# A one-core vision tower with eight experts: the scratch is cleared first, all expert rows are loaded at once, and the first experts' weights are asked for one after the other

## The reference

```
h = patchify(x) @ W_proj.T + b_proj + pos_emb          # 16 x 36 patches of 768 -> 256
h = concat(cls_tok, h)                                 # 16 x 37 = 592 tokens
h = h + attention(layernorm(h))                        # 16 heads of 16, causal, b_qkv, W_out, b_out
x = layernorm(h)
gates = softmax((x @ w_red) @ normalised(wg).T)        # 8 experts
e, score = argmax(gates), max(gates)
h = h + score * (gelu(x @ w1[e] + b1[e]) @ w2[e] + b2[e])   # 256 -> 1024 -> 256
```

## Time and profile before

| | us |
|---|---|
| median of 3 runs | 144.17 (144.15 to 144.57) |
| the profiled execution, its own time | 144.8 |
| its span, first to last recorded work | 143.0 |
| PE busy | 128.5 (90% of the span) |
| DVE, ACT, POOL busy | 58.2, 48.1, 41.0 |
| moved by DMA | 33.38 MB, mean 233 GB/s |

### The profile page before, as it was taken

How to read it: one execution, slowest core, us unless ns; L and a number is a source line. 1 busy time by engine, 2 the same in 40 slices (tenths; PEclk the granted TensorE clock), 3 DMA queues, 4 the chain that set the end, 5 groups by cost and what they waited for, 6 DMA issues and landing times.

```text
span 143.0 us, 2701 instructions
## 1 busy us (share of the span) xinstructions
PE 128.5 (90%) x1024; PEld 109.0 (76%) x1024; DVE 58.2 (41%) x179; ACT 48.1 (34%) x143; POOL 41.0 (29%) x53
## 2 busy tenths in 40 slices
PE   5999999999849999999879999992999999999970
PEld 2787888777536778777679988991899989999850
DVE  1012997619813788879847001600212111120210
ACT  0300004465712646562339350263006060505100
POOL 8600044900074093304637500040002020202022
PEclk9999999999995999999999999999689999999998
DMA  4999999948849999999104648885978799400000
GB/s 151 369 263 409 393 371 389 408 175 180 143 108 168 212 361 382 360 396 347 46 0 183 231 119 267 336 299 165 376 242 337 260 300 352 153 5 22 2 26 28
DMA packets 19790, 33.38 MB, mean 233 GB/s; under 512 B 1783, under 2 KB 13560, under 8 KB 19774
## 3 DMA queue, kind: packets, MB, share of 16 engines
q1 hardware_dynamic: 18238, 30.74, 65.9%
q0 software_dynamic: 768, 2.12, 4.1%
q10 hardware_dynamic: 768, 0.31, 1.3%
HBM read 27.76 MB, written 5.84 MB: 235 GB/s over the span
## 4 chain that ended last, share of the span: by engine, by line
PE 50%; DMA 27%; issue 8%; DVE 7%; SPq 3%; POOL 2%; ACT 1%; POOLq 0%
PE ps L810 13%; PE ps L796 10%; DMA out<-pos,early 8%; DMA early<-embed_in 6%; PE ps L528 5%; DMA w1s<-v_scratch 5%; DMA v_scratch<-hz 5%; DMA early<-slot_scratch 4%; PE ps L676 4%; PE ps L620 3%; PE ps L658 3%; PE ps L689 2%; PE ps L591 2%; PE ps L683 2%; SPq L309 2%
## 5 line engine op out<-in xcount | busy, mean ns | idle before, releaser
L511 ACT ACTIVATE early<-ps,b1s 128x128 f32<-128x128 f32 x64 | 18.2, 370 | 37.0 <-PE ps L796 32.1
L810 PE MATMUL ps<-w2s,early 128*128 128x256 f32 x128 | 30.5, 395 | 0.0
L796 PEld LDWEIGHTS ps<-early,w1s 128*128 128x128 f32 x256 | 29.4, 192 | 0.4 <-issue 0.2
L796 PE MATMUL ps<-early,w1s 128*128 128x128 f32 x256 | 29.6, 275 | 0.0
L810 PEld LDWEIGHTS ps<-w2s,early 128*128 128x128 f32 x128 | 25.0, 199 | 3.5
L1153 POOL DMA_INDIRECT out<-pos,early x8 | 7.8, 974 | 52.0 <-DVE pos L1076 51.7
L528 PE MATMUL ps<-early 128*128 128x256 f32 x60 | 14.9, 400 | 0.2 <-DMA early<-embed_in 0.2
L1060 DVE COPY early<-ps 128x256 f32<-128x256 f32 x6 | 2.5, 424 | 29.5 <-PE ps L779 29.5
L528 PEld LDWEIGHTS ps<-early 128*128 128x128 f32 x60 | 11.5, 199 | 2.5 <-DMA early<-embed_in 0.7
L1076 DVE SCALAR_TENSOR_TENSOR pos<-ps,early,hsum 128x256 f32<-128x256 f32 x8 | 3.9, 484 | 21.3 <-issue 21.2
L676 PE MATMUL ps<-vbd,probst 111*64 111x51 f32 (+2 forms) x192 | 6.7, 215 | 3.1 <-POOL vbd L1128 2.8
(11 more groups left out here) (130 smaller groups left out, 165.1 us busy)
## 6 DMA issues: line engine op xcount, KB each, us to landing
w1s<-w SPq DMA_DIRECT2D x8, 1024.0 KB, 8.2
w2s<-w SPq DMA_DIRECT2D x8, 1024.0 KB, 10.2
early<-embed_in SPq DMA_DIRECT2D x6, 448.0 KB, 6.4
slot_scratch<-nil SPq DMA_DIRECT2D x1, 2560.0 KB, 14.3
early<-slot_scratch SPq DMA_DIRECT2D x8, 320.0 KB, 4.7
b2s<-b SPq DMA_DIRECT2D x4, 256.0 KB, 7.7
wqkv<-w_qkv SPq DMA_DIRECT2D x1, 768.0 KB, 11.7
w1s<-v_scratch SPq DMA_DIRECT2D x3, 256.0 KB
```

What stands on the lines that cost most here:

```text
L511: nc.scalar.activation(gt[:, t % 2, f, :], ps[:, 2 * (t % 2) + f // 4, (f % 4) * P:(f % 4 + 1) * P], ACT.Gelu, bias=b1t[:, f:f + 1]).then_ ...
L796: m = nc.tensor.matmul(ps[:, 2 * (t % 2) + f // 4, (f % 4) * P:(f % 4 + 1) * P], w1s[:, r, k, f * P:(f + 1) * P], xt[:, t % 2, k, :], star ...
L810: m = nc.tensor.matmul(ps[:, 4 + t % 2, 0:D], gt[:, t % 2, f, :], w2s[:, r, f, :], start=(f == 0), stop=(f == FT - 1))
```

## The change

The places of the second scratch are cleared right after b_out, without expert 0's weights ahead of them; DVE fills the empty row (`nil`) before the gate's weights, not after. Expert 0's weights move behind the loads of the values; experts 1 and 2 are asked for only when those of the expert ahead have landed, then b2, then expert 3 after the last of the values was used, as before. All eight experts' rows are loaded right after the scattering: rows 4 to 7 have room of their own (`more`, behind place32 in `wide`), so no row load waits for an output scatter, and experts 4 to 7 wait for nothing but their slot. The mean is now taken off w_red by DVE, ahead of the product (three small instructions), so that L545 gives Gc at once, and L559, L881, L885 and `avg` go; the product with the bias takes a column of `boutc`, repeated over 128 columns, as its stationary operand. In the routing, `dispatch(2)` stands behind the second `count_before`.

```diff
+        more = wide[:, NT * ONCHIP * P:NT * ONCHIP * P + (E - RING) * ROW].rearrange("p (r n) -> p r n", r=E - RING)
...
+        def row_of(t):
+            r = t % E
+            return rows[:, r, :] if r < RING else more[:, r - RING, :]
...
-            load_expert(0)
             sp.dma_start(bout[:, :], b_out.partition_broadcast(P)).then_inc(q["loaded_bout"], 16)
             sp.wait_ge(q["nil_ready"], 2)
             sp.dma_start(of_expert[0:P, :, :], nil[:, :].unsqueeze(1).to_broadcast([P, E, ROW]))\
...
-            load_in_turn(1)
             sp.dma_start(iota[:, :], iota_d.partition_broadcast(P).rearrange("p o n -> p (o n)"))\
               .then_inc(q["loaded_iota"], 16)
             sp.dma_start(b1s[:, :, :], b1).then_inc(q["loaded_b1"], 16)
-            load_in_turn(2)
+            for t in range(RING - 1):
+                if t:
+                    sp.wait_ge(loaded_w[t - 1], 32)
+                load_expert(t)
+            sp.wait_ge(loaded_w[RING - 2], 32)
             for e in range(0, E, 2):
                 sp.dma_start(b2s[:, e:e + 2, :], b2[e:e + 2].partition_broadcast(P)).then_inc(q["loaded_b2"], 16)
             sp.wait_ge(q["v_ready"], PAIRS)
-            load_in_turn(RING - 1)
+            load_expert(RING - 1)
 
             def load_rows(t):
-                if t >= RING:
-
-                    sp.wait_ge(scattered[t % 2], 16 * ((t - RING) // 2 + 1))
-                sp.dma_start(rows[:, t % RING, :], of_expert[0:P, t, :]).then_inc(gathered[t % RING], 16)
+                sp.dma_start(row_of(t), of_expert[0:P, t, :]).then_inc(gathered[t], 16)
 
             sp.wait_ge(q["spread"], 16 * NT)
-            for t in (*range(ONCHIP, RING), *range(ONCHIP)):
+            for t in (*range(ONCHIP, RING), *range(ONCHIP), *range(RING, E)):
                 load_rows(t)
             for t in range(RING, E):
                 load_expert(t)
-                load_rows(t)
...
-                    pe.wait_ge(q["loaded_wred"], 16)
+                    pe.wait_ge(q["wred_ready"], 1)
...
-                if j == 0:
-                    pe.wait_ge(q["g_ready"], 1)
-                    pe.wait_ge(q["avg_ready"], 1)
-                    for k in range(KD):
-                        m = nc.tensor.matmul(mean_g, avg[:, :], G[:, k, :], start=(k == 0), stop=(k == KD - 1))
-                    m.then_inc(q["mean_ps"], 1)
...
-                    pe.wait_ge(q["gb_ready"], 1)
+                    pe.wait_ge(q["loaded_boutc"], 16)
                     for k in range(KD):
-                        m = nc.tensor.matmul(bo_ps, avg[:, :], Gb[:, k, :], start=(k == 0), stop=(k == KD - 1))
+                        m = nc.tensor.matmul(bo_ps, boutc[:, k:k + 1].to_broadcast([P, P]), Gc[:, k, :],
+                                             start=(k == 0), stop=(k == KD - 1))
...
-            for j in range(EARLY):
+            for j in range(EARLY - 1):
                 dispatch(j)
             count_before(EARLY, NT)
+            dispatch(EARLY - 1)
...
+            V.memset(nil[:, 2 * D + 1:ROW], 0.0).then_inc(q["nil_ready"], 1)
+            V.tensor_copy(nil[:, :].bitcast(U32)[:, 2 * D:2 * D + 1], C("norow")).then_inc(q["nil_ready"], 1)
+            V.tensor_copy(hz_id, C("tok")).then_inc(q["ids_ready"], 1)
+            dve.wait_ge(q["loaded_wred"], 16)
+            link(V.tensor_reduce(wmean[:, 0:1], wredt[:, :], AX.X, ALU.add))
+            link(V.tensor_scalar(wmean[:, 1:2], wmean[:, 0:1], -1.0 / D, None, ALU.mult))
+            V.tensor_scalar(wredt[:, :], wredt[:, :], wmean[:, 1:2], None, ALU.add).then_inc(q["wred_ready"], 1)
             dve.wait_ge(q["wgnt_ps"], 1)
```

More of the change, by code:

```diff
@@ L167, in vit_tower @@
         wredt = sb("wredt", [16, D])
-        G = sb("G", [P, KD, E])
-        avg = sb("avg", [P, P])
+        wmean = sb("wmean", [16, 2])
         woutt = sb("woutt", [P, KD, D])
@@ L295, in vit_tower @@
         scattered = [sem(f"scattered{b}") for b in range(2)]
-        gathered = [sem(f"gathered{r}") for r in range(RING)]
+        gathered = [sem(f"gathered{t}") for t in range(E)]
         block = ctx.enter_context(nc.Block())
@@ L367, in _ @@
             with sp.If(n > 0):
-                for r in range(RING):
-                    sp.wait_ge(gathered[r], 16 * E // RING)
+                for t in range(E):
+                    sp.wait_ge(gathered[t], 16)
                 for i in range(OVF):
@@ L387, in _ @@
                       .then_inc(loaded_w[r], 16)
-                    sp.wait_ge(scattered[(E + i) % 2], 16 * ((E + i - RING) // 2 + 1))
-                    sp.dma_start(rows[:, r, :], slot_d[bass.ds(row, P), :]).then_inc(gathered[r], 16)
+                    sp.wait_ge(scattered[i % 2], 16 * (i // 2 + 1))
+                    sp.dma_start(row_of(E + i), slot_d[bass.ds(row, P), :]).then_inc(gathered[i], 16)
             for b in range(2):
@@ L779, in turn_rows @@
                     m = nc.tensor.transpose(ps[:, 6 + t % 2, k * P:(k + 1) * P],
-                                            rows[:, t % RING, D + k * P:D + (k + 1) * P], ident)
+                                            row_of(t)[:, D + k * P:D + (k + 1) * P], ident)
                 m.then_inc(q["xt_ps"], 1)
@@ L1066, in result @@
                 b2t = tile_of(t)[2]
-                r = t % RING
-                dve.wait_ge(gathered[r], 16 * (t // RING + 1))
-                V.scalar_tensor_tensor(hsum[:, t % 2, :], b2t, row_score[:, r, :], rows[:, r, 0:D],
+                score = row_of(t)[:, 2 * D + 1:2 * D + 2]
+                dve.wait_ge(gathered[t % E], 16 * (t // E + 1))
+                V.scalar_tensor_tensor(hsum[:, t % 2, :], b2t, score, row_of(t)[:, 0:D],
                                        ALU.mult, ALU.add).then_inc(q["hsum_ready"], 1)
```

34 lines of the change are left out of this document (6 added, 28 removed).

## The result

The changed kernel takes 140.44 us (median of 4 runs, 139.66 to 141.1); the kernel before took 144.37 us (median of 4, 144.15 to 144.57). The ratio is 0.9726, with an interval of 0.9673 to 0.9779. The profiled run took 140.42 us with a span of 138.6 us. The forecast of 135.9 was 4.5 us too low, and its range ended at 140.1. The direction was right; of the 10.3 us to be won nearly all came, but the change took back 6.3 us at one place, where I had charged 1.0.

A forecast was written before the change was run, and what follows sets the result against it. PE was taken as the bound nearly everywhere (busy 90%), with gains where the chain of waits leaves it. Gains of 10.3 less 2.0 for two new stops gave 8.3 us off 144.17: 135.9 us, range 132.9 to 140.1.

The forecast's parts named there:

- The gains: Five terms over the whole kernel: embedding 0.3, stop before the values' first use 2.8, clock 1.3, routing 0.9, rows 5.0; sum 10.3 us.
- 4.1 (values and clock): Before the first `attend`: PE's stop for the value loads goes, 2.8 us, and its lowered clock behind it, 1.3 us.
- 5.0 (rows): Late experts: PE's stop for expert 4's rows, the slow `down` behind it and late turns go, 5.0 us.
- The waits' own times: Expert weight loads in turn: experts 0, 1 and 2 land at 51.9, 59.8 and 67.7 us, rounds of 7.9 us.
- the price of the stop at `turn_rows(2)`: At expert 2's rows: they come between 81.2 and 84.3, PE wants them at 82.5; stop 0 to 1.8, taken as 1.0 us.
- The term left out: PE's clock behind the two new stops: nothing added, as both were shorter than earlier ones; a drop would cost up to 1.7 us.
- Hidden 4: PE waits there for expert 4's weights, due between 96.2 and 100 and wanted at 96.6; stop 0 to 3.4, taken as 1.0 us.
- rival B: Scattering and rows pile up: stops of 1.8 + 2.5 us, clock falls once for 1.7, time 139.9; chance 0.17.
- A: No new stop: scattering done near 77.9, rows slip in, all 10.3 us come, time 133.9 down to 133.0; chance 0.2.
- C: The value store gets no faster, its own landing being slow; 2.8 + 1.3 us stay lost, time 140.0; chance 0.05.
- D: Slower than before: loading in turn starves the experts, from rounds of 11.7 us on; 146.8 at 13 us; chance 0.03.
- The rule on turns between the queues: DMA engines alternate packets between queues with work, so scattering and expert 3 slow each other, neither done much before 82.4 us.

## Why the prediction was wrong, point by point

**The gains** came. Both experiments that undid one of them gave a bit more than its term: 4.4 to 5.5 for 4.1 (values and clock), 5.6 for 5.0 (rows). The kernel without the waits has a span of 132.5, 10.5 us below the 143.0 of before, where I had summed 10.3. In the changed kernel's own trace: the store is issued at 24.99 and has landed at 27.79 (forecast 25.0 and 28.2); the value loads are there at 36.17, when POOL starts (36.6), and the second ones are issued at 36.37 (36.7); PE has no stop before the first `attend` and a clock of 1.00 from 40 to 50. DVE's second `keys` work runs from 67.05 with no wait. Hidden 0 starts at 70.06 (75.41 before), 5.35 us earlier; 0.3 + 2.8 + 1.3 + 0.9 = 5.3. That is the sum of four terms; the 0.3 and the 0.9 in it were not measured apart.

**The waits' own times** were right as well: expert 0 lands at 51.46 (51.9), expert 1 at 59.84 (59.8), expert 2 at 67.78 (67.7). The rounds of some 8 us that I took from the issue at 97.94 hold.

**The step that failed** is the price of the stop at `turn_rows(2)`: 1.0 us, measured 3.25. I had written that b2, expert 3 and the scattering are done at 82.4; the scattering was, at 82.65, but expert 3's second half only at 85.0. My way to the 82.4 was not sound either. The slices 20 and 21 that I named for a scattering with the DMA for itself end at 75.1, and its first bytes moved at 76.5; the rates while it ran are those of slices 22 to 24, 183, 231 and 119 GB/s, not 370. So the landing at 82.65 is near my figure partly by luck. What made the price wrong comes after it: I put expert 2's rows between 81.2 and 84.3. The lower end had the scattering land undisturbed at 77.9, with the 3.3 us of a load behind it. The upper end let the rows slip in behind expert 3 as 0.9 us of data and 1 us of landing. Neither goes with a scattering that is done at 82.4. SP waits for its landing before it issues any row, and what is issued after that pays its whole time: 82.65 + 3.17 = 85.82. With my own 82.4 the sum would have been 82.4 + 3.3 = 85.7 against 82.5 for PE, a stop of 3.2; measured 3.25.

**The term left out** depends on it. I had added nothing for the clock, because both stops were to be shorter than those of the earlier trace rows. At 3.25 us it is longer, the clock fell to 0.50, and this cost 3.1 by the chain in the profiled run and 2.4 against the experiment that keeps PE busy. Together 3.25 + 3.1 = 6.35 instead of 1.0.

**Hidden 4** had a term of 1.0 and no stop. The row loads were issued 4.7 us later than I had them, but PE was later still, by 6.35, and its weights were there at 101.75. So that term was swallowed, as I had said only of rival B. Where PE came sooner it shows: with w1 of expert 3 early, PE waits 0.58 us for expert 4 at 97.97. The 10.9 us that I gave eight row loads there doesn't follow from its rows: four of them took 8.3 us (82.96 to 91.3), expert 4's part included, and I didn't say what I took off.

The balance: 5.35 more at turn 2, 1.0 less at hidden 4, which makes 4.35 of the 4.5 us that were missing.

**The rivals.** B (the scattering and rows pile up, 139.9) is the one that happened, at 0.17. Its mechanism was right, its parts weren't: one stop of 3.25 and not 1.8 + 2.5, and 3.1 for the clock instead of 1.7. The 1.7 was `down` alone (5.30 against 3.62); here hidden 2 and 3 ran slow too (8.05 against 7.31). A is what comes without the waits: 134.3 for a forecast of 133.9 (its lower end adds up to 132.9, as in the range, and not to 133.0). C didn't happen, and for D the rounds were never near 11.7 us.

**The rule on turns between the queues.** For six us, from 69 to 75, the trace doesn't show turns: q1 moved 1.49 MB and q0 nothing. From 77 to 79 it shows them packet for packet, 73 of q0 and 70 of q1 in one us, 77 and 74 in the next, and since q0's packets are larger it then had 72% and 78% of the engines' time. By the Trainium skill, "DMA: Bandwidth & Descriptors", section "Queues, rings and completion order", an engine takes a packet from each queue that has work in turn. With the second stretch the trace agrees, and the first it fits only if POOL's packets were not ready for the engines until 75, which no run here shows. Nor does it show turns with b2 asked for ahead of expert 0, where q0 moved 1 and 2 packets from 76 to 78 and q1 83 and 132.

**What stays open** is why the scattering starts so late. The first bytes moved 1.8 to 1.9 us after the first issue where SP had at most some 1 MB left to move (before, the kernels without waits, expert 3 behind the rows), and 4.5 to 5.9 us after it where b2 and all or half of expert 3 were asked for by then and 1.1 to 1.8 MB of SP's went first (changed kernel, PE kept busy, last wait dropped, either half of expert 3 early). In these last the scattering landed at 80.96 to 82.65. Where expert 3 was asked for amid it, it had begun after 1.7 and 2.6 us, at 71 to 72, and yet landed last (83.45, 83.61). The size of the packets doesn't explain it, and the bytes alone don't either.

## What to carry to other kernels

A wait in a DMA queue moves every byte behind it to a later time: before such a wait is put in, look what those bytes will meet there. Here 3.15 MB met a scattering of 1.5 MB on whose landing all rows wait, and 6 us were gone; with no wait all but 0.15 MB of the same loads was through when the scattering was issued. And a load that is issued on a landing pays its whole time after that landing (3.17 us for expert 2's rows): write both times down for each such link, and price the clock with the stop.

## What the runs showed of the hardware

- The clock fell behind the longer of PE's stops. Behind stops of 1.49 and 1.86 us it stayed at about 1.00. In each of the profiled runs with a stop of 2.29, 2.39, 2.62, 2.96, 3.25, 3.47, 3.95 or 4.25 us it was 0.50 for some us from the stop on. What that costs doesn't go with the length of the stop: 2.9 us behind 3.25 and 1.9 behind 3.47 (against the kernel without the waits). And it doesn't come in every run: with expert 3 behind the rows, two of four runs kept a mean of 0.998 and 1.000.
- Two DMA queues with work don't always add up: 214 GB/s from 76 to 79 us where expert 3 was asked for amid the scattering, 413 GB/s in the same three us of the changed kernel.
- POOL's indirect DMAs moved no byte for 4.5 to 5.9 us after their first issue where SP had b2 and expert 3 (or half of it) queued, and started after 1.9 us where it was b2 alone. Why, no run shows.
- One expert asked for behind four row loads and with more behind it took 11 us to land (80.56 to 91.8), while one alone in SP's queue took 7.9 to 8.4 (51.46 to 59.84, and 59.84 to 67.78).
